# A Flamingo stack on one core: tables of beats of their own for each lane, and the values of two units of the small attentions multiplied in one visit

## What is computed

```python
x = x + tanh(g_xattn[0]) * attention_16_heads(layernorm(x), ctx, ctx, mask)          # small attention 0
x = x + tanh(g_ffn[0])   * mixture_8_experts_top2_and_shared(layernorm(x))           # first mixture
x = x + tanh(g_xattn[1]) * attention_16_heads_with_biases(layernorm(x), ctx, ctx)    # small attention 1
x = x + tanh(g_ffn[1])   * switched_attention(layernorm(x))  # 16 heads of 64, 8 value experts, top 2 in and out
x = x + tanh(g_xattn[2]) * mlstm_4_heads(layernorm(x), ctx, ctx)
x = x + tanh(g_ffn[2])   * bit_linear_conv_silu(layernorm(x))
x = x + tanh(g_xattn[3]) * wide_attention_with_ffn(layernorm(x), ctx, ctx)
x = x + tanh(g_ffn[3])   * mixture_16_experts_top4_and_shared(layernorm(x))          # last mixture
```

## Time and profile before

| | us |
|---|---|
| runs | 2517.3, 2514.52, 2517.75 |
| median | 2517.3 |
| the profiled execution, time | 2514.25 |
| the profiled execution, span | 2512.2 |
| PE busy in it | 2196.2 |
| DVE busy | 1748.2 |
| ACT busy | 1282.0 |
| POOL busy | 141.0 |

### The profile page before, as it was taken

The page is one execution under the profiler, slowest core; times in us unless marked ns, Lnnn a source line. Parts: engine busy times, 40 slices in busy tenths (PEclk is TensorE's granted clock), DMA queues, the critical chain, the costliest instruction groups (busy, mean ns, idle before and its releaser), DMA issues.

```text
span 2512.2 us, 50619 instructions
## 1 busy us (share of the span) xinstructions
PE 2196.2 (87%) x19506; PEld 1569.4 (62%) x19506; DVE 1748.2 (70%) x5567; ACT 1282.0 (51%) x3714; POOL 141.0 (6%) x180
## 2 busy tenths in 40 slices
PE   7998889988899888998889988899888998899887
PEld 3667556675567755676556765557655576555765
DVE  6864777757777477774877757777487775777657
ACT  4365354654446544474444734447344473444734
POOL 0000100001000010000000011000110001100010
PEclk9999999999999999999999989999899998999999
DMA  4034000330004300042000520005100051000510
GB/s 168 1 92 96 17 5 1 99 88 18 5 1 105 82 17 5 1 117 70 18 5 1 134 53 20 3 1 139 48 20 3 1 139 48 20 3 8 145 35 5
DMA packets 312512, 115.45 MB, mean 46 GB/s; under 512 B 268752, under 2 KB 295376, under 8 KB 312016
## 3 DMA queue, kind: packets, MB, share of 16 engines
q1 hardware_dynamic: 312272, 112.23, 17.5%
HBM read 63.96 MB, written 48.23 MB: 45 GB/s over the span
## 4 chain that ended last, share of the span: by engine, by line
PE 43%; DVE 32%; DMA 8%; ACT 7%; issue 5%; POOL 4%; SPq 1%; DVEq 0%; ACTq 0%
PE banks L408 6%; PE banks L344 5%; ACT PP L820 4%; PE banks L463 3%; DVE nm L1160 3%; PE banks L547 3%; POOL mv L1699 2%; PE banks L341 2%; DMA va<-o_d 2%; DVE qk L1241 2%; PE banks L502 2%; PE banks L294 2%; DVE xn L1072 2%; PE banks L680 2%; DVE st L1065 2%
## 5 line engine op out<-in xcount | busy, mean ns | idle before, releaser
L820 ACT ACTIVATE PP<-banks,nm 128x128 f32<-128x128 f32 x1568 | 444.8, 396 | 220.7 <-DVE nm L1160 124.5
L1160 DVE TENSOR_REDUCE nm<-banks 128x4 f32<-128x512 f32 (+1 forms) x400 | 261.2, 675 | 177.7 <-PE banks L344 122.0
L408 PE MATMUL banks<-w_sb,PP 128*128 128x128 f32 x1536 | 247.1, 285 | 61.3 <-ACT PP L820 28.9
L294 PE MATMUL banks<-identb 128*128 128x256 bf16 x1408 | 237.5, 283 | 24.8 <-ACT PP L975 22.4
L408 PEld LDWEIGHTS banks<-w_sb,PP 128*128 128x128 f32 x1536 | 166.1, 142 | 148.0 <-issue 55.6
L1699 POOL TENSOR_TENSOR mv<-mv,half 128x2 f32<-128x2 f32 x160 | 112.8, 705 | 2197.9 <-DVE mv L1057 2197.9
L1203 DVE COPY PP<-banks 128x512 f32<-128x512 f32 x256 | 175.5, 690 | 63.5 <-PE banks L408 60.1
L463 PE MATMUL banks<-w_sb,qk 128*128 128x128 f32 x1280 | 178.0, 278 | 2.2 <-DVE qk L1304 1.3
L294 PEld LDWEIGHTS banks<-identb 128*128 128x128 bf16 x1408 | 135.6, 102 | 65.1 <-ACT PP L975 30.1
L463 PEld LDWEIGHTS banks<-w_sb,qk 128*128 128x128 f32 x1280 | 161.8, 192 | 18.7 <-issue 11.4
L811 ACT ACTIVATE xnT<-banks 128x256 f32<-128x256 f32 x128 | 49.2, 384 | 229.6 <-PE banks L302 229.6
(11 more groups left out here) (283 smaller groups left out, 4339.1 us busy)
## 6 DMA issues: line engine op xcount, KB each, us to landing
va<-v_d SPq DMA_DIRECT2D x32, 512.0 KB, 5.5
o_d<-oa SPq DMA_DIRECT2D x64, 256.0 KB, 3.5
va<-o_d SPq DMA_DIRECT2D x32, 512.0 KB, 4.4
pv_d<-PP SPq DMA_DIRECT2D x32, 256.0 KB, 3.5
oa<-pv_d SPq DMA_DIRECT2D x32, 256.0 KB, 3.1
v_d<-PP SPq DMA_DIRECT2D x16, 512.0 KB, 3.9
v_d<-tmp SPq DMA_DIRECT2D x16, 512.0 KB, 6.1
w_sb<-weights SPq DMA_DIRECT2D x1, 5599.0 KB, 23.5
```

Source lines behind the costliest of these rows:

```text
L294: pe.matmul(bank(k, n)[:, cols(c, T)], identb[:, :], bc(identb[:, :], 1, G), start=True, stop=True, skip_group_check=True)
L408: e = pe.transpose(bank(k, 2)[:, cols(j)], P[k][:, 512 * (u % 2) + 128 * j:][:, 0:128], ident)
L820: e = act.activation(P[k][:, 512 * (u % 2) + 128 * j:][:, 0:128], bank_[:, cols(j)], ACT.Exp, bias=nm[k][:, m:m + 1])
L1160: e = dve.tensor_reduce(m, b3(scores[:, 0:maps * 128], maps), AX.X, ALU.max, negate=True)
```

## The change

1. `SHIFT` goes, and each table of beats becomes two, one for each lane. For DVE the second is the first plus 1339, which is the order of before. For PE the second is the old table plus 1339, and the first is new. For ACT, POOL and SP both are new. The merged order that follows is the same as before on DVE and POOL; it differs on PE, ACT and SP.
2. `values` of an even unit issues its spares and returns. That of an odd unit waits for the copy of its own unit and issues the matmuls of both, with an increment of `o_ps` after each unit.
3. The turned maps have four buffers, `PT4`: two in `PT`, two in `tmp`. The copy of unit n waits for the values of unit n - 4.
4. The load of `pick` lands in `mixd` of lane 1, not in `tmp` of lane 0.
5. The 101 numbers of `SPARES` are new. Their sum was 88 and is 115.

The counts by place that change most, before and after, in one lane's turn: small attention 0, ahead of the key and value projections 0, 3; query projection 3, 0; fifth turned maps 3, 0; output transposes 0, 7. First mixture: turned rows 3, 8; gates 1, 3. Small attention 1: key and value projections 3, 0; third turned maps 5, 0; third unit's values 0, 4. Switched attention: turned rows 0, 5; gates 4, 0; second mixing 1, 5; second output mixing 4, 0. mLSTM: first and second decay maps 10 and 0, 1 and 3; turned products 6 and 4, 8 and 3. Convolution: turned rows 0, 9. Wide attention: output transposes 5, 0; second normed rows 1, 8. Last mixture: turned rows 2, 9; logits 0, 3; gates 3, 1.

```diff
@@ -34,28 +34,50 @@
-TURN, SHIFT = 39873, 1339
-BEATS_PE = (
-    -2214, -466, -461, -93, 353, 697, 798, 1052, 1382, 1480, 1551, 1551, 1551, 1815, 2124, 2305, 2673, 2829, 3076, 3148,
...
-BEATS_ACT = (
-    -1669, -1595, -1563, -870, -870, -48, 249, 809, 1052, 1838, 1838, 2035, 2440, 3223, 3538, 4257, 4346, 4346, 4346, 4439,
...
-BEATS_DVE = (
+TURN = 39873
+BEATS_PE = ((
+    -1250, -612, -326, -44, 358, 653, 679, 1059, 1283, 1395, 1454, 1561, 1923, 2116, 2199, 2211, 2316, 2889, 2917, 2958,
...
+), (
+    -875, 873, 878, 1246, 1692, 2036, 2137, 2391, 2721, 2819, 2890, 2890, 2890, 3154, 3463, 3644, 4012, 4168, 4415, 4487,
...
+BEATS_ACT = ((
+    -8966, -8251, -7832, -7583, -6570, -3813, -3813, -1707, -1592, -971, -454, -454, -222, 931, 2243, 2777, 2777, 3064,
...
+), (
+    -6332, -5569, -4104, -2684, -2087, -1000, -969, -276, -254, -143, 593, 957, 2673, 3911, 5819, 6433, 7433, 7433, 8409,
...
+BEATS_DVE = ((
...
-BEATS_SP = (
-    -178284, -178284, -178193, -178193, -177326, -177326, -177326, -177009, -177009, -176487, -175517, -168289, -168289,
-    -167984, -167955, -167955, -167775, -166618, -166580, -166580, -160674, -145843,)
+BEATS_SP = ((
+    -242752, -242553, -242553, -238131, -238131, -237804, -237804, -237058, -236981, -233923, -230618, -221598, -219346,
+    -218796, -217615, -212325, -212215, -209270, -206607, -206485, -203699, -203699,
+), (
+    -235003, -231213, -230164, -229008, -229008, -228143, -225901, -221262, -221262, -221262, -221262, -218853, -213790,
+    -209157, -209065, -206564, -205345, -205168, -204765, -204680, -203168, -203066,
+))
 
 SPARES = (
-    0, 0, 3, 0, 0, 2, 0, 0, 0, 0, 0, 3, 0, 1, 0, 0, 0, 1, 0, 0, 0, 0, 3, 0, 1, 1, 3, 0, 0, 0, 0, 0, 0, 5, 0, 0, 0, 0, 0, 0,
-    0, 0, 0, 0, 2, 0, 0, 0, 0, 4, 0, 3, 1, 1, 0, 0, 0, 0, 0, 1, 0, 0, 0, 0, 0, 0, 0, 0, 0, 0, 0, 4, 0, 0, 0, 0, 10, 0, 6, 4,
-    0, 0, 8, 0, 0, 0, 5, 0, 0, 0, 0, 0, 4, 5, 1, 1, 0, 2, 0, 3, 0,)
+    3, 1, 0, 0, 1, 0, 0, 0, 0, 0, 0, 0, 0, 0, 0, 0, 0, 0, 0, 1, 7, 0, 8, 0, 3, 0, 0, 0, 0, 0, 0, 0, 0, 0, 0, 0, 4, 0, 0, 0,
+    0, 0, 0, 0, 0, 2, 1, 0, 5, 0, 0, 1, 5, 0, 0, 0, 0, 0, 0, 0, 0, 0, 0, 0, 0, 0, 0, 0, 0, 0, 1, 0, 0, 0, 0, 2, 1, 3, 8, 3,
+    0, 9, 8, 0, 0, 0, 3, 0, 0, 2, 2, 3, 4, 0, 3, 8, 0, 9, 3, 1, 0,
+)
 
 
 XN_A0, XN_M0, XN_A1, XN_SW, XN_ML, XN_CF, XN_WA, XN_WA2, XN_M3 = range(9)
@@ -92,7 +134,7 @@
     heads = []
     for k, lane in enumerate(lanes):
         next(lane)
-        heads.append([k * SHIFT + beats[0], k, 0, lane])
+        heads.append([beats[k][0], k, 0, lane])
     while heads:
         head = min(heads, key=lambda h: h[:2])
         _, k, n, work = head
@@ -101,8 +143,8 @@
         except StopIteration:
             heads.remove(head)
             continue
-        turn, chunk = divmod(n + 1, len(beats))
-        head[0], head[2] = k * SHIFT + turn * TURN + beats[chunk], n + 1
+        turn, chunk = divmod(n + 1, len(beats[k]))
+        head[0], head[2] = turn * TURN + beats[k][chunk], n + 1
 
 
 class Signal:
@@ -248,8 +290,9 @@
         gs, gm, gt = (pair(n, G * 256) for n in ("gs", "gm", "gt"))
         tmp, PP = pair("tmp", 1024), pair("PP", 2048)
         P, PT = [p[:, 0:1024] for p in PP], [p[:, 1024:2048] for p in PP]
+        PT4 = [[PT[k][:, 0:512], PT[k][:, 512:1024], tmp[k][:, 0:512], tmp[k][:, 512:1024]] for k in range(LANES)]
         mixd, seld = pair("mixd", G * TG * 64), pair("seld", G * 2 * TG * 32)
-        pick_ld = tmp[0][:, 0:E3 // 2 * 128]
+        pick_ld = mixd[1][:, 0:E3 // 2 * 128]
         mixc, selc = [g[:, 0:256] for g in gt], [g[:, 256:512] for g in gt]
         pv1, pvR = P, [o[:, 1024:2048] for o in oa]
         vr = [(PT[k], tmp[k][:, :]) for k in range(LANES)]
@@ -350,12 +393,14 @@
                     pe.wait_ge(ov_ok[k], ov_ok.n(i, 2 * s))
                 if g < 3:
                     spare(pe, k, 3, 1)
+                if g % 2 == 0:
+                    return
                 pe.wait_ge(pT_ok[k], pT_ok.n(i, 8 * s + u))
-                for j in range(HQ):
-                    e = pe.matmul(bank(k, 3)[32 * j:32 * j + 32, cols(g)], v4[:, b, HQ * g + j, :],
-                                  PT[k][:, 512 * (u % 2) + 128 * j:][:, 0:128], start=True, stop=True,
-                                  tile_position=(0, 32 * j))
-                e.then_inc(o_ps[k], 1)
+                for n in (u - 1, u):
+                    for j in range(HQ):
+                        e = pe.matmul(bank(k, 3)[32 * j:32 * j + 32, cols(n % 4)], v4[:, b, HQ * (n % 4) + j, :],
+                                      PT4[k][n % 4][:, cols(j)], start=True, stop=True, tile_position=(0, 32 * j))
+                    e.then_inc(o_ps[k], 1)
 
             def turn_out(b):
 
@@ -1198,9 +1243,9 @@
                     for n in (u - 1, u):
                         yield
                         dve.wait_ge(pT_ps[k], pT_ps.n(i, 8 * s + n))
-                        if n >= 2:
-                            dve.wait_ge(o_ps[k], o_ps.n(i, 8 * s + n - 2))
-                        dve.tensor_copy(PT[k][:, cols(n % 2, 512)], bank(k, 2)).then_inc(pT_ok[k], 1)
+                        if n >= 4:
+                            dve.wait_ge(o_ps[k], o_ps.n(i, 8 * s + n - 4))
+                        dve.tensor_copy(PT4[k][n % 4], bank(k, 2)).then_inc(pT_ok[k], 1)
                 next(late, None)
             yield
             dve_small_out(dve, k, i, s, 0)
```

11 lines of the change are left out of this document (9 added, 2 removed), and 60 rows, old and new, of tables (BEATS_ACT, BEATS_DVE, BEATS_PE).

## The result

| | before | after |
|---|---|---|
| median, us | 2516.5 (4 runs) | 2456.8 (4 runs, 2454.35 to 2459.81) |
| ratio, 95% interval | | 0.9764, 0.9747 to 0.9781 |
| profiled span, us | 2512.2 | 2454.6 |

The change makes the kernel 2.4% faster, 60 us; the forecast was 14 us, and the time is outside its range. From here on "single visits" means values as they were before (one unit in a visit, two buffers), and "pairs" the new form.

The account below looks back on a forecast made before the run. The bound was taken to pass from engine to engine, with PE busiest and no single wait carrying the time. The terms -10 + 2 + 12 - 14 - 4 = -14 us gave 2503 us, 0.6% faster, range 2468 to 2536 us.

Parts of the forecast that it names:

- Part 3, order: Switched attention: ACT's and SP's new orders shorten chains through DMAs, 1.7 us a turn, 14 us saved; ends -32 and +16.
- two waits that I read as signs of the order: Switched attention, lane 1: PE idle 1.63 us behind ACT's copy and 1.35 us ahead of the mixing matmuls, for ACT's spread.
- ACT second: Switched attention: lane 0's second copy, exponentials and first turned copy come ahead; before, ACT idled 1.76 us, PE 1.35 us.
- SP first: Switched attention: earlier mask and third output writes start lane 1's chain up to 1.7 us earlier, lane 0's some 3 us.
- Part 2, spares: Whole turn: 432 more spares, some not covered by PE's waits, cost 12 us; +36 us net if the order stays.
- Part 4, clock: Convolution, wide attention, decay maps: spares change low-clock time, 100 us in all; 4 us saved, ends -17 and +10.
- Part 1, pairs: Small attentions: values of two units in one visit save 10 us of PE, ends 0 and 17.
- The delayed gather: Small attentions: the last pair delays the gather at the end of each half by about 0.2 us; 2 us taken.
- (a): Rival: spares are paid where PE arrives without a wait, no gain in the order; 2539 us, chance 0.20.
- (b): Rival: nothing is left, saved visits become waits for exponentials, order's gain lost in the mLSTM; 2514 to 2520 us, chance 0.14.
- (c): Rival: DMA chains were the bound, 4 us a turn comes and small attentions give 17 us; 2480 us, chance 0.17.
- (d): Rival: the clock stays at 2.4 GHz throughout, so half of the 100 us goes; 2457 us, chance 0.05.

Follow-up runs that it names:

- sp_order_alone: The kernel before with only SP's new tables of beats; ratio 1.0017 to the kernel before.
- old_sp_order: The changed kernel with SP's old tables of beats; ratio 0.9761 to the kernel before.
- spares_alone: The kernel before with only the new 101 numbers of spares; ratio 1.0037 to the kernel before.
- orders_alone: The kernel before with the new tables of PE, ACT, POOL and SP, values and spares as before; ratio 0.9903 to the kernel before.
- old_values: The changed kernel with single visits and two buffers, new orders and new spares kept; 2442.4 us, ratio 0.9723 to the kernel before.
- old_pe_act_order: The changed kernel with PE's and ACT's old tables of beats, SP's new; ratio 1.0122 to the kernel before.
- single_again: The changed kernel with single visits and two buffers, run once more side by side with the changed kernel; ratio 0.9745 to the kernel before.
- values_alone: The kernel before with only the values of two units in one visit and four buffers; ratio 1.0056 to the kernel before.

## Why the prediction was wrong

- The sign was right, the size wrong by 46 us, and the likeliest mechanism wrong. Three of the four terms (pairs, spares, clock) came out with the other sign in the changed kernel, so the right sign of the sum is partly luck. What was right in small: the bound passes from engine to engine, and the gain was all PE's idle time.
- Part 3, order, -14 us with ends -32 and +16: the step that failed is to look for the order's worth only where "ACT and SP change in earnest, in the switched attention". I had looked at PE's order, found that it "swaps pairs of neighbouring steps", and given it nothing. The runs show something else: PE's and ACT's order is worth 2.3% by stretches, over half of it in the small attentions and the first mixture, where I saw no order term at all. By order alone small attention 0 became 1.6 us a turn shorter and small attention 1 1.35 us, with nothing at the lower clock, and PE's wait for the exponentials fell from 28.9 to 10.8 us. Small moves were the gain there.
- The two waits that I read as signs of the order did move, but against each other. PE's and ACT's order takes the wait for the spread away, as "ACT second" said; SP's new order takes the wait for the copy away, as "SP first" said, and brings the one for the spread back. I had written down this risk ("if ACT is late there, lane 1's whole mixing chain is") and kept it as an end of 2 us a turn. By itself SP's order gives 3.3 us a turn at the end of the switched attention and takes 4.4 us ahead of it (`sp_order_alone` 1.0017, `old_sp_order` no different from the changed kernel).
- Part 2, spares, +12 us, and +36 us if the order stays: the old order had 9 us, and the new one 46 to 50 us of gain. The step that failed is pricing spares by what lies uncovered in the timeline of before. Even in the old order its largest item, 0.96 us for the nine ahead of lane 0's convolution rows, costs nothing: from these rows to the wide attention lane 0 takes 18.88 us before and 17.89 us in `spares_alone`, both at the full clock, and lane 1's rows, for which PE waits in both, come 9.4 and 8.4 us behind lane 0's. In the new order it is the old spares that stand in the way, and the clock, which the new ones hold better, was a term of its own of -4 us.
- Part 4, clock. Its price of low time, 0.27 of the length, was read from six matmuls of the convolution; the stretch that holds them loses 0.41, and other stages 0.33 to 0.65 (next section). What was wrong is the amount at stake. By (1 - clock) x 2 x span I counted the 100 us at the lower clock in the kernel before as what could be won. But the new order with the old spares runs 167 us at the lower clock, and without spares (1 - 0.931) x 2 x 2522.8 = 348. What the spares do is prevent, not win back.
- The two together close, as an estimate. Orders alone against `old_values` is 7.1 us a turn. Of it, 1.1 us are, by their count, the five old spares ahead of the wide attention's output transposes (27.8 against 26.7 us, both at the full clock; 2 lanes x 5 x 0.11 = 1.1). 1.0 us is small attention 0, also at the full clock. The rest goes with 12 us a turn more at the lower clock (19.3 against 7.4), at some 0.4 us each 4.8 us. Sum 6.9.
- Likewise the order's own worth: orders alone is 2.9 us a turn faster than before, with 8.5 us more at the lower clock (3.4 us) and the 2.1 us of spares that are now in the way: 8.4 us a turn, 67 us in eight, if the spares fit it.
- Part 1, pairs, -8 us: the size of a visit was right (busy time of values down 23 us, sixteen matmuls in 0.65 us as in the earlier trace rows; of the 2.5 us by which PE's busy time in small attention 0 fell in the fifth turn, 1.3 are the pairs', 40.6 us against 41.8 in `old_values`), and it was worth less than nothing, 6 to 14 us lost. The failed step is the line "PE is busy nine tenths of this stage": the visits that went stood, where the timelines were read, in the other tenth. The delayed gather, for which I took 2 us, shows in the output transposes' wait, 5.1 us for 0.6. That four buffers by themselves give nothing was right.
- PE's busy time was to rise by 20 to 45 us and rose by 5: the added spares cost busy time, and the pairs and the clock in the convolution gave it back.
- Rivals: (a) is the case of `old_pe_act_order`, not of this kernel. (b) is out. (c) was to show by a span over 30 us shorter at the same clock and busy time, and that came; it was no proof, since the order of PE and ACT gives the same picture. (d) has by chance the time that was measured, 2457, but the clock did not stay at 2.4 GHz: the profiled execution has 130 us at the lower one, for 100 before.
- The best kernel of the study is the change without its pairs, single visits with new orders and spares: 2442 to 2444 us, 0.9723 and 0.9745.

## What to carry to other kernels

Price the order of the engine that is the bound first: many small moves carried more than the one long chain through a queue that was easy to see. Filler work on TensorE (here the spares) and the order of work are one term and not two: filler that fits one order costs in another, and an order tested with the old filler shows a third of its worth. A merged visit saves time only where the engine has none to spare at the place of the visit that goes; look at that place, not at the busy share of the stage.

## What the runs showed of the hardware

Matmuls that nobody reads, put where TensorE waits, raise the granted clock so much that the program gets shorter: 0.931 without spares, 0.980 with 1840, and 80 us. What a microsecond at 1.2 GHz costs can be read from turns of one kernel:

| stretch | kernel | without | with low clock | cost per us |
|---|---|---|---|---|
| small attention 1, lane 0 | after | 45.23 | 48.40, 6.83 us low | 0.46 |
| convolution, lane 0 | before | 18.88 | 20.29, 3.41 us low | 0.41 |
| wide attention, lane 0 | orders alone | 27.77 | 28.88 to 29.10 and 30.36, 3.41 and 6.83 low | 0.33 to 0.39 |
| switched attention, first scores to first values | before | 23.4 (five turns, 22.98 to 23.88) | 25.63, 3.41 low | 0.65 (0.51 to 0.78) |

The price depends on where the low stretch falls. In the mLSTM, first decay map to convolution, every turn of `old_values` takes 26.5 us, four with 3.41 us low and four with 6.83: the second 3.41 us cost nothing. The turns of `old_sp_order` with 10.2 to 12.9 us low take 28.0 to 28.7 us, 0.35 to 0.45 for each us beyond 6.83. In turn 8 of the kernel before the convolution has 4.93 us low and takes 18.90, no longer than without. The two kernels' means (26.52 us with 5.12 low, 28.19 with 11.38) give 0.27, the number of the prediction, by the mix of both. The Trainium skill, "TensorE: Matmul & The Clock Gate", section Terms, puts the penalty at the throttled time times one minus the clock's share, 0.5 at half the clock; these rows have from nothing to 0.46 in most stages, and 0.65 in the switched attention.

Where the low stretches fall differs from one execution to the next: `old_values` and `single_again` are the same kernel, with 96 and 143 us of it, and spans of 2433.4 and 2442.4 us. A difference of two profiled spans below 10 us says nothing here; the ratios and the stages at the full clock do.

The orders' effect in a stage of the fifth turn, wide attention, shows both costs in one line, `orders_alone` and then the changed kernel:

```profile
1502.10:1531.00 28.90, 23.61 (x157) 18.17 (x155) 18.09 (x69) 10.95 (x27) 3.57 (x5) 0.94 0.04 12
```

```profile
1487.80:1514.50 26.70, 24.74 (x184) 19.48 (x182) 18.11 (x69) 10.97 (x27) 3.58 (x5) 1.00 0.04 12
```

PE does 27 instructions more in it, nearly all spares, and is through 2.2 us earlier: 1.1 us by the spares that moved and 1.1 us by the clock (`orders_alone` takes 27.8 us there in its turns at the full clock).

What stays open: which of the moves in the small attentions is worth what (only stretches were tried), by which DMA SP's new queue makes the spread late, and where the rest of the 14 us of `values_alone` goes, of which the stages at the full clock show 4. The pairs' cost, 0.41% in one comparison and 0.25% in the other, is known only to about that difference.
